# Sliding-window attention block with LoRA experts, fp32, one core: values applied in two 64x64 turns, layer norms moved behind the projections, one probability norm moved to GpSimd

## The reference

```python
q, k, v = x @ wq.T, x @ wk.T, x @ wv.T          # of layernorm(x), per head
q, k = rmsnorm(q, q_norm_w), rmsnorm(k, k_norm_w)
...
mask = (i >= j) & (i - j < WIN)
attn = softmax(where(mask, q @ k.T / 8, -inf))
x = x + (attn @ v) @ wo.T
...
h = layernorm(x)
gate = softmax(h @ gate_w.T)                     # 8 experts, rank 16
x = x + h @ weight.T + (1 / 16) * lora(gate, lora_V, h @ lora_U.T)
```

## Time and profile before

| what | value |
|---|---|
| time, median of 3 runs | 2423.46 us (2421.21 to 2423.61) |
| profiled execution, its own time | 2420.27 us |
| its span in the trace | 2418.6 us |
| granted TensorE clock, mean | 0.996 of 2.4 GHz |
| PE, ACT, DVE, POOL busy | 98%, 89%, 89%, 54% |
| tiles | 128, so some 18.5 us each |

### The profile page before, as it was taken

The page is one execution under the profiler, slowest core; times in us unless marked ns, Lnnn a source line. Parts: engine busy times, 40 slices in busy tenths (PEclk is TensorE's granted clock), DMA queues, the critical chain, the costliest instruction groups (busy, mean ns, idle before and its releaser), DMA issues.

```text
span 2418.6 us, 70409 instructions
## 1 busy us (share of the span) xinstructions
PE 2380.1 (98%) x25856; PEld 1958.6 (81%) x25856; DVE 2152.0 (89%) x5736; ACT 2160.9 (89%) x7687; POOL 1309.6 (54%) x1771
## 2 busy tenths in 40 slices
PE   6999999999999999999999999999999999999997
PEld 4888888888888888888888888888888888888886
DVE  6899899999988999999999899989999998999886
ACT  5899989999998999899989989998999899899996
POOL 3555555555555555555555555555555555555542
PEclk9999999999999999999999999999999999999999
DMA  2000000000000000000000000000000000000000
GB/s 70 13 15 19 15 15 16 18 15 15 19 15 15 15 19 15 15 15 19 15 15 19 16 15 15 19 15 15 15 20 15 15 17 18 15 15 19 13 9 12
DMA packets 39729, 41.23 MB, mean 17 GB/s; under 512 B 4448, under 2 KB 38624, under 8 KB 39392
## 3 DMA queue, kind: packets, MB, share of 16 engines
q1 hardware_dynamic: 39392, 36.73, 5.0%
HBM read 19.93 MB, written 16.78 MB: 15 GB/s over the span
## 4 chain that ended last, share of the span: by engine, by line
PE 97%; issue 1%; ACT 1%; POOL 1%; DVE 1%; DMA 0%; SPq 0%; POOLq 0%
PE ps_a L633 17%; PE ps_scores L676 14%; PE ps_y L695 12%; PE ps_d L629 7%; PE ps_d L627 7%; PE ps_d L628 7%; PE ps_y L710 5%; PE ps_b L629 5%; PE ps_b L627 5%; PE ps_b L628 5%; PE ps_d L633 3%; PE ps_c L629 2%; PE ps_c L628 2%; PE ps_c L627 2%; PE ps_c L633 1%
## 5 line engine op out<-in xcount | busy, mean ns | idle before, releaser
L330 ACT ACTIVATE probs<-merged,neg_max 128x128 f32<-128x128 f32 x2048 | 796.0, 394 | 0.5 <-DVE neg_max L491 0.5
L253 POOL TENSOR_SCALAR_AFFINE_SELECT pT_other<-pT 128x256 f32<-128x256 f32 x384 | 173.1, 451 | 606.4 <-ACT pT L345 606.4
L237 POOL TENSOR_TENSOR q_r<-q_ve,minus_half 128x8 f32<-128x8 f32 x256 | 420.3, 1642 | 92.4 <-DVE q_ve L467 92.4
L676 PE MATMUL ps_scores<-kT,qT 64*64 64x192 f32 (+2 forms) x8192 | 415.2, 311 | 1.0 <-DVE merged L481 0.6
L330 ACT ACTIVATION_READ_ACCUMULATOR probs<-merged,neg_max 128x1 f32 x2048 | 396.5, 194 | 0.0
L481 DVE COPY_PREDICATED merged<-later_key,ps_scores 128x512 f32<-128x512 int32 x384 | 284.7, 741 | 106.2 <-ACT merged L323 106.2
L345 ACT ACTIVATE pT<-ps_a 128x512 f32<-128x512 f32 x512 | 306.2, 598 | 62.0 <-PE ps_a L633 61.1
L491 DVE TENSOR_REDUCE neg_max<-merged 128x4 f32<-128x512 f32 x512 | 346.5, 677 | 4.5
L695 PE MATMUL ps_y<-pT,values 128*64 128x128 f32 x4096 | 337.0, 285 | 1.8 <-ACT pT L345 1.8
L633 PE MATMUL ps_a<-ident,probs 128*128 128x128 f32 x2048 | 336.4, 287 | 0.0
L676 PEld LDWEIGHTS ps_scores<-kT,qT 64*64 64x64 f32 x8192 | 262.7, 133 | 60.6 <-issue 32.8
(11 more groups left out here) (114 smaller groups left out, 6175.7 us busy)
## 6 DMA issues: line engine op xcount, KB each, us to landing
xs<-x SPq DMA_DIRECT2D x128, 128.0 KB, 2.2
out<-ob SPq DMA_DIRECT2D x128, 128.0 KB, 1.7
w_plain<-w_qkv SPq DMA_DIRECT2D x3, 512.0 KB, 5.0
w_plain<-w_o SPq DMA_DIRECT2D x8, 128.0 KB, 5.3
w_plain<-w_ffn SPq DMA_DIRECT2D x1, 392.0 KB, 5.7
w_plain<-w_v SPq DMA_DIRECT2D x1, 128.0 KB, 4.9
nw<-norm_w SPq DMA_DIRECT2D x1, 1.0 KB, 5.5
```

The source lines that it names most:

```text
L237: pool.tensor_tensor(q_r[:, T % DEEP, c], q_ve[:, T % DEEP, c], minus_half[:, 0:8], ALU.pow).then_inc(s_qr[n], 1)
L330: last = nc.scalar.activation(probs[:, r, h], merged[:, r, h], ACT.Exp, bias=neg_max[:, r, h:h + 1], accum_out=den[:, r, h:h + 1])
L676: last = nc.tensor.matmul(ps_scores[queries, 2 * half + c, first:end], qT[rows, T % 2, 2 * g + c, queries], kT[rows, g // 2, at + first:at ...
```

## The change

It has four parts. **Values in two turns.** `attend` becomes `attend_across` and `attend`, each of four fp32 matmuls in 64*64. `attend_across` takes the keys of the half that is opposite to the query half, `attend` those of the same half; both add into the same banks, so the first must be over before the second starts (semaphore `pv_across_done`), and another group's `scores` are put between them. `attend_other` follows. **Layer norms behind the projections.** At the start PE multiplies the three pieces of `w_qkv` and `w_ffn` by a constant 1/256 matrix, which gives the mean over the input rows in PSUM, and DVE subtracts it (`centre_weights`) before the split into high and low. With such weights the mean of x drops out. So raw `xs` and raw `x1` are transposed; `x_rstd` scales only the values, as the scale of ACT's copies in `store_v`; for q and k it drops out in their own norm, whose epsilon becomes `x_eps` (one more DVE instruction a tile). For the second norm `h_rstd` enters in the gate's maximum (`gate_max_normed`, one more), as the scale of the gate's exponential and in `add_x1`. `centre_x` and `norm_x` (POOL) and `norm_h` (DVE) go. **One probability norm by GpSimd.** `normalise` goes from ACT; `norm_by_pool` does group 2 in one 128x512 instruction. **A new order** of every queue and another sharing of banks a to d.

```diff
-NORM_BY_ACT = (2,)
+NORM_BY_POOL = (2,)
...
-            def centre_x(T):
-                    pool.tensor_tensor(xc[:, T % DEEP], xs[:, T % WIDE], x_mv[:, T % DEEP, 0:1].to_broadcast([P, DIM]), ALU.subtract).then_inc(s_xc, 1)
...
-            def norm_x(T):
-                    pool.tensor_tensor(xn[:, T % DEEP], xc[:, T % DEEP], x_rstd[:, T % DEEP].to_broadcast([P, DIM]), ALU.mult).then_inc(s_xn, 1)
...
+            def norm_by_pool(T, g):
+                if live(T):
+                    r = ring(T, g)
+                    pool.wait_ge(s_rden, groups(T, g))
+                    pool.tensor_tensor(probs[:, r], probs[:, r], rden[:, r].unsqueeze(2).to_broadcast([P, REP, P]), ALU.mult).then_inc(s_pnp, 1)
...
-            def normalise(T, g):
-                    for h in range(REP):
-                        last = nc.scalar.activation(probs[:, r, h], probs[:, r, h], ACT.Copy, scale=rden[:, r, h:h + 1])
...
+            def centre_weights(k):
+                dve.wait_ge(s_wm, k + 1)
+                w = plain(CENTRED[k])
+                nc.vector.tensor_tensor(w, w, mean_bank(k).unsqueeze(1).to_broadcast(w.shape), ALU.subtract).then_inc(s_wc, 1)
...
+                    nc.vector.tensor_scalar(x_eps[:, T % DEEP], x_mv[:, T % DEEP, 1:2], RMS_EPS, LN_EPS * RMS_EPS, ALU.mult, ALU.add).then_inc(s_xeps, 1)
...
-                    nc.vector.tensor_scalar(hn[:, T % 2], x1[:, T % DEEP], h_mv[:, T % DEEP, 0:1], h_rstd[:, T % DEEP], ALU.subtract, ALU.mult).then_inc(s_hn, 1)
...
+                    nc.vector.tensor_tensor(g_negmax[:, T % DEEP], g_neg[:, T % DEEP], h_rstd[:, T % DEEP], ALU.mult).then_inc(s_gmax, 1)
...
-                    nc.vector.tensor_tensor(ob[:, T % 2], ps_ffn[:, 0:DIM], x1[:, T % DEEP], ALU.add).then_inc(s_ob, 1)
+                    nc.vector.scalar_tensor_tensor(ob[:, T % 2], ps_ffn[:, 0:DIM], h_rstd[:, T % DEEP], x1[:, T % DEEP], ALU.mult, ALU.add).then_inc(s_ob, 1)
...
-            def attend(T, g, first=True):
-                for n in range(2):
-                    for half in range(2):
-                        last = nc.tensor.matmul(ps_y[HD * half:HD * half + HD, n, 0:P], values[:, T % WIDE, g // 2 * 2 + half],
-                                                pT[:, ring(T, g), 2 * half:2 * half + 2, HD * n:HD * n + HD], start=first, stop=ends, skip_group_check=True)
+            def attend_across(T, g):
+                for half in range(2):
+                    for n in range(2):
+                        keys = slice(HD - HD * n, P - HD * n)
+                        last = nc.tensor.matmul(ps_y[HD * half:HD * half + HD, n, 0:P], values[keys, T % WIDE, g // 2 * 2 + half],
+                                                pT[keys, ring(T, g), 2 * half:2 * half + 2, HD * n:HD * n + HD], start=True, stop=False, skip_group_check=True)
+                last.then_inc(s_px, 1)
...
+            def attend(T, g, last=False):
+                pe.wait_ge(s_px, groups(T, g))
+                        keys = slice(HD * n, HD * n + HD)
...
+            def weight_means(k):
+                for c in range(KC):
+                    last = nc.tensor.matmul(mean_bank(k), mean_of[:], w[:, c], start=c == 0, stop=c == KC - 1)
```

More of the change, by code:

```diff
@@ L191, in _ @@
                 load_x(T)
-            for T in range(TILES):
+            for T in range(TILES + 2):
                 load_x(T + WIDE)
-                sp.wait_ge(s_ob, done(T))
-                sp.dma_start(out[T * P:(T + 1) * P, :], ob[:, T % 2]).then_inc(s_st[T % 2], 16)
+                store(T - 2)
             for n in range(2):
@@ L690, in attend, with attend_other @@
                     pe.wait_ge(s_v, done(T))
-                first = first or not slot(T)
-                ends = not first or not slot(T)
-                for n in range(2):
-                    for half in range(2):
-                        last = nc.tensor.matmul(ps_y[HD * half:HD * half + HD, n, 0:P], values[:, T % WIDE, g // 2 * 2 + half],
-                                                pT[:, ring(T, g), 2 * half:2 * half + 2, HD * n:HD * n + HD], start=first, stop=ends, skip_group_check=True)
+                    if T == 0:
+                        pe.wait_ge(s_wc, len(CENTRED))
+                for half in range(2):
[6 more added lines that the diff above has]
+                pe.wait_ge(s_px, groups(T, g))
+                ends = last or not slot(T)
+                for half in range(2):
+                    for n in range(2):
+                        keys = slice(HD * n, HD * n + HD)
+                        end = nc.tensor.matmul(ps_y[HD * half:HD * half + HD, n, 0:P], values[keys, T % WIDE, g // 2 * 2 + half],
+                                               pT[keys, ring(T, g), 2 * half:2 * half + 2, HD * n:HD * n + HD], start=False, stop=ends, skip_group_check=True)
                 if ends:
-                    last.then_inc(s_pv, 1)
-            def attend_other(T, g, first=False):
+                    end.then_inc(s_pv, 1)
+            def attend_other(T, g, last=False):
                 if not slot(T):
                     return
+                pe.wait_ge(s_px, groups(T, g))
                 pe.wait_ge(s_po, later_groups(T, g))
@@ L709, in attend_other @@
                         keys = slice(HD * n, HD * n + HD)
-                        last = nc.tensor.matmul(ps_y[HD * half:HD * half + HD, n, 0:P], v_diff[keys, T % RING, g // 2 * 2 + half],
-                                                pT_other[keys, ring(T, g), n, 2 * half:2 * half + 2], start=first, stop=not first, skip_group_check=True)
-                if not first:
-                    last.then_inc(s_pv, 1)
+                        end = nc.tensor.matmul(ps_y[HD * half:HD * half + HD, n, 0:P], v_diff[keys, T % RING, g // 2 * 2 + half],
+                                               pT_other[keys, ring(T, g), n, 2 * half:2 * half + 2], start=False, stop=last, skip_group_check=True)
+                if last:
+                    end.then_inc(s_pv, 1)
             def project_out(T, g):
@@ new lines, in step @@
+                if live(T - 2):
+                    attend(T - 2, 2)
+                if live(T - 2):
+                    attend_other(T - 2, 2, last=True)
+                if live(T - 3):
+                    freed(pe, (s_ob, T - 4, done(T - 4)), (s_qT[0], T - 1, done(T - 1)), (s_htl, T - 4, done(T - 4)))
+                    transpose_h(T - 3)
+                if live(T):
+                    freed(pe, (s_ttl, T - 4, done(T - 4)), (s_xtl, T + 1, done(T + 1)), (s_kT, T - 1, done(T - 1)), (s_kn, T - 1, done(T - 1)))
+                    project_kv(T)
@@ new lines, in step @@
+                if live(T - 2):
+                    attend(T - 2, 3)
+                if live(T - 2):
+                    attend_other(T - 2, 3, last=True)
+                if live(T):
+                    freed(pe, (s_htl, T - 3, done(T - 3)), (s_ob, T - 4, done(T - 4)), (s_qT[0], T - 1, done(T - 1)))
+                    transpose_q(T, 0)
+                if live(T + 1):
+                    freed(pe, (s_pT, T - 1, groups(T - 1, 0)), (s_pT, T - 2, groups(T - 2, 3)), (s_pT, T - 2, groups(T - 2, 2)), (s_pT, T - 2, groups(T - 2, 1)), (s_qn[0], T, done(T)))
+                    project_q(T + 1, 0)
```

367 lines of the change are left out of this document (183 added, 184 removed).

## The result

The changed kernel takes 2370.19 us (median of 4, 2369.13 to 2371.09), the one before 2423.53 beside it (2421.21 to 2423.72): 0.978 of the time, 95% interval 0.9765 to 0.9799. That is faster, inside the whole range, and 20 us above the forecast of 2350. It is also outside the 2338 to 2362 that the forecast's own case allowed, and inside the 2363 to 2400 of rival A. The profiled execution took 2369.13 us, its span 2367.4.

A forecast was written before the change was run, and what follows sets the result against it. TensorE's instruction stream was taken to bound the kernel: span 2418.6 - 76.8 (values) + 6.0 (start) - 0.4 (end) = 2347.4 us, 2349 with time outside the span; forecast 2350, range 2338 to 2405.

The forecast's parts named there:

- forecast's own case: Whole kernel: PE without regular waits, forecast 2350 us, own range 2338 to 2362; chance 0.60.
- rival A: PE begins to wait 0.1 to 0.4 us a tile, 13 to 50 us come back: 2363 to 2400; chance 0.23.
- What bounds the kernel: Kernel before: bound by TensorE's instruction stream, 18.5 us a tile; the other engines' idle time is slack.
- Values in 64*64: PE's visits to smaller shapes: 0.27, 0.65, 0.22, 0.32, together 1.46 against 1.61 us; 76.8 us in all.
- Rival D: The change of shape is not what costs, so the pace stays: 2429 us; chance 0.04.
- rival C: Row tiles in 64*64 hinder each other, rounds of values 0.22: 225 us more, 2575; chance 0.01.
- The new steady pace: Four tiles in 71.6 us instead of 73.99; tightest chain, from q's first-half projection to `low_y`, has 0.3 us slack.
- rival B: GpSimd's long product holds up DVE's two-SBUF-input instructions: 2376, or 2484 with more stalls; chance 0.12.
- One norm by POOL: Norm moved from ACT: ACT loses 163.0 us, worth nothing alone; POOL's 128x512 product taken as 1.38 us.
- Norms behind the projections: PE's stream unchanged; DVE net nothing, 66.9 us for four tiles; POOL loses two instructions of 0.69.
- The start: First projection at 22.8 us instead of 16.84, after means and centring: 6.0 us later, bounds 0 and 9.
- The end: Last tile's chain loses 0.4 us without `hn`.

The follow-up runs named there:

- experiment 1: Changed kernel with `gate_share` moved two instructions earlier in DVE's queue, ahead of group 2's `inverse`, which releases GpSimd's norm: 2354.12 us.
- experiment 4: Changed kernel with values in full rows (128*64) again, the first turn doing all four matmuls, the second none: 2433.54 us.
- experiment 2: Changed kernel with GpSimd's 128x512 norm issued as two halves of 128x256, order unchanged: 2354.59 us.
- experiment 3: Changed kernel with the norm of group 2 back on ACT, behind `store_pT` of group 1: 2380.34 us.

## Why the prediction was right and where it was wrong

**What bounds the kernel: right.** PE without regular waits at 73.98, then again at 71.63 in experiment 1. The whole range and the sign hold; that the time falls into the range is in part the width that rival A gave it.

**Values in 64*64: right, to the hundredth.** 0.27, 0.65, 0.22, 0.32 in the trace; experiment 4 takes it away and loses 63 us again, with visits of 1.62. Rival D is out by that, rival C by the rounds of 0.11.

**The new steady pace: the step that failed.** It laid out the chain projection, square, sum, `merge`, `low_y` with 0.3 us of slack, and wrote of the rest "Elsewhere I find 0.5 us or more". That chain, which ends in `low_y` of group 3, held. The wait came at the next `low_y`, of group 0. What failed is a duration on DVE: `gate_share` does not appear in the working, so it was left at what it took before (247 ns in the mean), and takes 712, in front of `merge`. It is held in three of four tiles; in two of these the block ahead of `attend_across` takes 1.79 us instead of the 1.61 of experiment 1, and in one of the two the next transpose of the gated experts takes 0.07 more: 0.43 of the 0.5 in four tiles, worked out from block lengths. A hold of 0.68 that costs PE 0.18 leaves a slack of some 0.5 there (an estimate from these numbers), as the prediction had it; the term that it put at nothing ate it. Of its signs of being wrong, a wait for `yT_l` is the one that came. This is rival A's size (0.13 us a tile, 2370) by rival B's mechanism. I had given A 0.23 and B 0.12 as two cases; they were one. B's text weighed only instructions with two SBUF inputs and so looked at norms and `v_diff`. `v_diff` indeed won, as written; its mean even fell from 612 to 422 ns. The instruction behind it lost.

The row tells it first: an instruction with one tensor input in SBUF and its output there, 0.22 alone, 0.90 behind GpSimd's start. The trace of the kernel before had it too, in a smaller size. GpSimd's select and VectorE there, in order of time:

```profile
1100.49 0.41 POOL L253 TENSOR_SCALAR_AFFINE_SELECT pT_other<-pT 128x256 f32<-128x256 f32 x1 [2.25 <-ACT pT L345]
...
1100.61 0.32 DVE L552 TENSOR_SCALAR gate<-g_exp,g_rden 128x8 f32<-128x8 f32 x1
```

`gate_share` ends at 1100.93, 0.03 after the select, in 31 of the 128 tiles; alone it takes 0.22. Its mean of 247 ns was a mixture of the two. The page "SBUF — State Buffer" of the Trainium skill (Who interferes with whom) has a second rule, which I passed over: `tensor_scalar` is among the operations that can enter a mode that also takes the port pair shared with GpSimd, and whoever issues first has that pair for its whole instruction. By that rule this trace agrees, 712 against 222 ns, and by its "whole instruction" experiment 2 does, with 398. That the mode is the reason is what the Trainium skill says; the runs show the hold and where it ends.

**One norm by POOL: its length was 1.22 us** (mean of L251; I took 1.38 between 0.73 and 1.38). That too is a mixture: 1.27 in the 96 tiles where DVE's `v_diff` started just before it, 1.04 in the 32 without a `v_diff`. Its worth was mis-stated. "Off the path, worth nothing alone" holds at the old pace, not at the new one: experiment 3 against 1 gives 26 us. ACT lost less than the 163 us that I wrote, 101 by the page: its copies with a scale from memory are longer. `values` of 64x256 go from 378 ns to 470, the gate's exponential from 267 to 343, 33 us in all over their 384 instructions; the other 29 are spread over groups and overlaps that I did not separate.

**Norms behind the projections, net nothing on DVE: right** in sum (66.54 for four tiles, forecast 66.9), but partly by luck: the hold of `gate_share`, which the forecast did not have, is 2.0 of them (the gate's eight instructions take 3.91 there, 1.93 in experiment 1), and experiment 1 has 65.76 in all.

**The start: right in size** (+5.7 against +6.0). **The end: wrong, +2.4 by the cut at q's first half (1.7 for filling and draining without a cut) instead of -0.4.** I counted the `hn` that goes, and not what the drain lacks. TensorE in order of time, the last tiles:

```profile
2341.40 0.45 PE L714 MATMUL ps_y<-pT,values 64*64 64x128 f32 x8
2341.93 0.45 PE L725 MATMUL ps_y<-pT,values 64*64 64x128 f32 x8
```

Without `scores` between them the second turn starts 0.53 after the first, where two rounds take 0.27. That is the price that the working named (0.2 a visit, here 0.26) and did not apply to the last tile's four visits: 1.0 us, and the waits have it as 1.3 in four. The rest fits the new sharing of banks: the transpose of raw `x1` and the last ffn share bank c with the output's sum, so they follow each other. It also fits the new order, which has the last projection of q's first half ahead of one more visit than before. Which of the two it is was not tested.

## What to carry to other kernels

Read where every short DVE instruction stands when GpSimd gets a longer one, and not only those with two inputs: one of eight numbers a row cost 16 us here, and moving it ahead of the instruction that releases GpSimd gave all of it back. Where a mean duration of such an instruction lies above its shortest, look at the single ones: the collision may be there already. An engine off the critical path has a slack that belongs to the pace; work out its worth at the new pace, not at the old one. And a saving on the bounding engine comes out in full only if the queues around it are laid out for the faster pace: the same 77 us gave 30 in the old order.

## What the runs showed of the hardware

A DVE `tensor_scalar` of 128x8 fp32 from SBUF to SBUF takes 0.22 us alone and is held to the end of a GpSimd product that started before it (0.90 seen). One of 128x1 keeps its 154 ns in the mean in the same trace, a `copy_predicated` with PSUM on one side and a `v_diff` that started first are not held. In the kernel before, a select of 0.41 us holds the one of 128x8 to 0.32. GpSimd's 128x512 product with a broadcast factor takes 1.04 us by itself and 1.27 where DVE's `v_diff` started first; a half of 128x256 takes 0.61 and 0.85. An ACT copy of 64x256 takes 0.09 us more with a per-row scale from memory. A stretch in 128*64 between work of other shapes cost 0.15 us beyond its rounds (visits of 1.62 and 1.47 us): that is what the kernel saves by giving up its third shape.
